# Summing the rows read back behind the last scatter: fp32 products instead of three bf16 parts

## The reference

```python
# layer 2
msg = norm[:, None] * x[col]
agg = jax.ops.segment_sum(msg, row, num_segments=n)
out = relu(agg @ W.T + b)
# layer 3
msg = gate * h[dst] * (cw * mj)[:, None]
agg = jax.ops.segment_sum(msg, src, num_segments=N)
tot = jax.ops.segment_sum(mj, src, num_segments=N)
# after each layer
x = _layernorm(x + layer(x))
```

## Time and profile before

| | |
|---|---|
| median of 3 runs | 16765.21 us (16758.88 to 16766.94) |
| the profiled execution's own time | 16730.78 us |
| its span, first to last instruction | 16728.8 us |
| mean granted TensorE clock | 0.629 |
| PE, DVE, ACT, POOL busy | 71%, 54%, 20%, 74% |

### The profile page before, as it was taken

One profiled execution on the slowest core, in us unless ns is written; L12 is line 12 of the kernel. 1 busy time (PEld: TensorE's weight loads), 2 busy tenths in 40 slices (PEclk: granted clock), 3 DMA queues, 4 the chain that ended last, 5 costly groups with the idle time before them and its releaser, 6 DMA issues. The chain is left out here.

```text
span 16728.8 us, 275034 instructions
## 1 busy us (share of the span) xinstructions
PE 11888.0 (71%) x58162; PEld 10815.9 (65%) x58163; DVE 9022.7 (54%) x22074; ACT 3298.4 (20%) x9767; POOL 12345.1 (74%) x12756
## 2 busy tenths in 40 slices
PE   7777888777666666666533498988853339888884
PEld 6777777777544444444433488888843338888884
DVE  4666667666544444444422266666662226666667
ACT  1111111111211111111111111111123333333332
POOL 4777777777777777777677777777757777777775
PEclk9999999999555555555555555555555555555555
DMA  5444444444333333333211122222221112222222
GB/s 130 101 100 101 101 101 101 100 101 96 87 83 84 86 85 83 86 84 84 66 41 41 48 74 72 75 73 73 74 55 47 47 51 79 78 80 79 78 79 54
DMA packets 1447655, 1320.81 MB, mean 79 GB/s; under 512 B 958662, under 2 KB 1304425, under 8 KB 1443052
## 3 DMA queue, kind: packets, MB, share of 16 engines
q0 software_dynamic: 450320, 493.60, 12.8%
q1 hardware_dynamic: 502094, 520.02, 12.7%
q10 hardware_dynamic: 495148, 306.20, 6.4%
HBM read 903.35 MB, written 415.31 MB: 79 GB/s over the span
## 5 line engine op out<-in xcount | busy, mean ns | idle before, releaser
L1507 POOL DMA_INDIRECT order<-l_msg,l_uring x6250 | 6052.9, 968 | 1918.1 <-issue 1845.9
L1683 PE MATMUL ps<-l_win,l_oht 32*128 x12500 | 2729.9, 413 | 1990.6 <-DMA l_win<-htab 823.3
L1683 PEld LDWEIGHTS ps<-l_win,l_oht 32*128 32x128 f32 x12500 | 2684.1, 327 | 2031.9 <-issue 2031.9
L489 POOL DMA_INDIRECT l_rows<-btab,l_sd x3125 | 3006.0, 962 | 1126.1 <-issue 1084.5
L1027 POOL DMA_INDIRECT l_rows<-y,l_sd x3125 | 2985.7, 955 | 966.5 <-issue 922.3
L1659 PE MATMUL ps<-l_ordb,l_ohs 128*128 128x49 f32 x13600 | 2967.0, 414 | 318.3 <-DVE l_ohs L1552 135.1
L1659 PEld LDWEIGHTS ps<-l_ordb,l_ohs 128*128 128x128 f32 x13600 | 2922.6, 332 | 367.3 <-issue 280.3
L1571 DVE TENSOR_TENSOR acc<-acc,ps 128x49 f32 x7520 | 1525.1, 206 | 1294.5 <-issue 718.6
L630 PE MATMUL ps<-l_rhs,l_lhs 64*128 x6250 | 1422.0, 423 | 676.9 <-DVE l_rows L566 471.8
L630 PEld LDWEIGHTS ps<-l_rhs,l_lhs 64*128 64x128 f32 x6250 | 1350.9, 328 | 738.5 <-issue 738.5
L645 PEld LDWEIGHTS ps<-l_ohe,l_hid 128*128 128x128 f32 x6250 | 1342.9, 332 | 34.9 <-issue 34.1
(11 more groups left out here) (255 smaller groups left out, 11238.0 us busy)
## 6 DMA issues: line engine op xcount, KB each, us to landing
l_ordb<-order SPq DMA_DIRECT2D x752, 250.0 KB
order<-l_msg,l_uring POOLq DMA_INDIRECT x6250
order<-l_zero ACTq DMA_DIRECT2D x125, 775.0 KB, 4.5
l_dstb<-ids SPq DMA_DIRECT2D x376, 200.0 KB
l_eat<-in_ea40P SPq DMA_DIRECT2D x125, 600.0 KB
gates<-l_gate ACTq DMA_DIRECT2D x125, 600.0 KB
l_gin<-gates SPq DMA_DIRECT2D x125, 600.0 KB
l_rows<-btab,l_sd POOLq DMA_INDIRECT x3125
```

Source lines behind the costliest of these rows:

```text
L489: pool.indirect_dma_start(rows[:, t, :], None, d["btab"], bass.IndirectOffsetOnAxis(ap=sd[:, t, 0:1], axis=0)).then_inc(gat[c], 16)
L1507: pool.indirect_dma_start(d["order"], bass.IndirectOffsetOnAxis(ap=uring[:, t:t + 1], axis=0), msg[:, t, :], None).then_inc(sc[c], 16)
L1683: done = t.matmul(look[c][:, j, :], oht[:, c * CE + j * P:c * CE + (j + 1) * P], win[:, ds((w % 2) * SET + c * LW, LW)], start=False, stop ...
```

## The change

The tail uses the functions of the main loop. The split, its four steps on ACT and POOL, their semaphores, the bf16 digits, the bf16 products and SP's separate load are gone. The nine steps run `load_order`, `block_digits`, `block_reduce` and `block_sums`, in the same order on each engine. The main loop isn't touched.

```diff
-        ohsb = [ohs[b][:, 0:RB[b] // 2, :].bitcast(BF16).rearrange("p k (j n) -> p (k j) n", n=P) for b in range(len(RB))]
-        spare = agg[:, 2 * WIDE:pl.NP].bitcast(BF16)
-        parts = [spare[:, 3 * first[b] * MW:3 * (first[b] + RB[b]) * MW].rearrange("p (i k f) -> p i k f", i=3, f=MW) for b in range(len(RB))]
...
@@ sync
-            def load_last(n):
-                ...
-            with sp.Fori(TAIL0, TAIL0 + 1) as n:
+            with sp.Fori(NG - READ0, pl.NS) as n:
                 load_order(n)
-            with sp.Fori(TAIL0 + 1, pl.NS) as n:
-                load_last(n)
@@ gpsimd
-            with pool.Fori(TAIL0, pl.NS) as n:
-                ... less_hi, less_mid
@@ vector
             with dve.Fori(NG - READ0, pl.NS) as n:
-                last_digits(n, 0)
+                block_digits(n, 0)
                 block_sums(n - 1, LAST)
-                last_digits(n, 1)
+                block_digits(n, 1)
                 block_sums(n, 0)
-                last_digits(n, 2)
+                block_digits(n, 2)
                 block_sums(n, 1)
-                last_digits(n, 3)
+                block_digits(n, 3)
                 block_sums(n, 2)
@@ tensor
-            with pe.Fori(TAIL0, pl.NS) as n:
+            with pe.Fori(NG - READ0, pl.NS) as n:
                 for b in range(len(RB)):
-                    last_reduce(n, b)
+                    block_reduce(n, b)
@@ scalar
-            with act.Fori(TAIL0, pl.NS) as n:
-                ... take_hi, take_mid
```

More of the change, by code:

```diff
@@ L1392, in scatter_pass @@
         ohs = [s.sb(f"ohs{b}", [P, RB[b], P]) for b in range(len(RB))]
-        ohsb = [ohs[b][:, 0:RB[b] // 2, :].bitcast(BF16).rearrange("p k (j n) -> p (k j) n", n=P) for b in range(len(RB))]
-        assert all(k % 2 == 0 for k in RB) and 2 * (pl.NP - 2 * WIDE) >= 3 * RT * MW
-        spare = agg[:, 2 * WIDE:pl.NP].bitcast(BF16)
-        parts = [spare[:, 3 * first[b] * MW:3 * (first[b] + RB[b]) * MW].rearrange("p (i k f) -> p i k f", i=3, f=MW) for b in range(len(RB))]
-        hi_made, rest_made, mid_made, lo_made = (s.sem(k) for k in ("hi_made", "rest_made", "mid_made", "lo_made"))
-        TAIL0 = NG - READ0
         ids_in = s.sem("ids_in")
@@ L1552, in block_digits @@
                 v.tensor_tensor(ohs[b][:, :, :], bc(count_row[:, None, :], [P, RB[b], P]), bc(lo, [P, RB[b], P]), ALU.is_equal).then_inc(ohs_ready, 1)
[L1554 to L1559, removed]
             def block_sums(n, b):
@@ L1660, in block_reduce @@
                                     ordb[b][:, k, 0:MW], start=True, stop=True)
[L1661 to L1670, removed]
                 done.then_inc(red_ready, 1)
```

## The result

The changed kernel takes 16723.13 us (median of 14 runs, 16718.25 to 16729.48), against 16758.75 us for the kernel before in 14 runs beside it (16755.34 to 16766.94). The ratio is 0.9978, 95% interval 0.9971 to 0.9985: **36 us faster**. I had forecast 22 us slower, 16787, and a range from 16770 to 16802; the forecast was wrong in sign.

The account below looks back on a forecast made before the run. DVE was taken to bound the tails now, PE after the change. Each tail: 1.73 + 149.45 + 1.6 + 4.63 + 1.77 = 159.2 us against 148.3; twice 10.9 gave 21.8 slower, 16787 us from 16765.21, range 16770 to 16802.

Parts of the forecast that it names:

- PE becomes the tail's bound at 4.27 us a block: Nine steps after the last scatter, layers 2 and 3: fp32 blocks take 4.27 us on PE against DVE's 4.03.
- The clock: TensorE's granted clock in the tails: taken to stay at 0.50, that is 1.2 GHz.
- the rival in which it comes back: Tail at 2.4 GHz: about 2.2 us a block, DVE bounds, time stays 16765; chance 0.06, shared with PE hidden otherwise.
- Four passes of 49 columns, 0.163 us a product: Counter-estimate for tail products: 1.6 us a block, hidden under DVE, time unchanged; the measured block was preferred.
- Closings: PE's pause where the tail's loop closes: 0.2 us a step taken, bounds 0 and 0.68, 8 closings a stage.
- The tail's part: First digits to last adds: 159.2 us a stage against 148.3, 10.9 longer, 21.8 us for both stages.
- Loads of rows, registers: Tail: row reloads hidden by 7 us of slack; address loads need some 1.86 us and have 2.2 at least.
- I cost its removal at nothing, because DVE's adds hide it: Tail: 144 roundings off ACT and 144 subtractions off POOL, some 240 us of work, priced at 0.
- far from the tail: Sign of being wrong: stages far from the tail shift; given no size or chance.
- GpSimd leaves DVE alone: Rival: without POOL's subtractions DVE's tail adds speed up, 29 us, 16736; chance of faster 0.02.

Follow-up runs that it names:

- half of the products: Changed kernel with PE making five of a block's ten products in the nine tail steps: 24334.69 us, ratio 1.0020 to the kernel before.
- the second set: Changed kernel (16701.70 us) and it with unused semaphores (16705.07), memsets (16700.52) or subtractions on POOL (16759.88), beside the kernel before (16733.16).
- the split by additions: Kernel before, its bf16 split kept but ACT negating and POOL adding instead of subtracting: 16678.30 us (ratio 0.9967); at the other pace 24344.22 (1.0020).
- fifth sets: Split by additions (16678.30 us) and changed kernel with eight POOL subtractions in layer 3 alone (16699.69), beside the kernel before (16732.85).

## Why the prediction was wrong

- **PE becomes the tail's bound at 4.27 us a block**: right. Adds that waited for PE in the step above start 4.27 to 4.57 apart, PE is 97% busy, and half of the products free DVE again.
- **The clock**: 0.50 in both tails, with PE 97% busy; the rival in which it comes back is out. The rule that activity releases the halved clock (the Trainium skill, TensorE: Matmul & The Clock Gate, What's actually happening) isn't borne out by these two tails.
- **Four passes of 49 columns, 0.163 us a product** (an estimate from the count of passes in the Trainium skill, FP8 and Floating Point Precision, TensorE Precision Notes): a product took 0.427 us here too (adds at 12289.51 and 12293.78, ten products apart), as the row of before had said.
- **Closings**: 17.43 - 4 x 4.27 = 0.35 a step in layer 2 and 0.45 in layer 3, taken as 0.2. The weight loads pause 0.29 there. With it the tails come to 160.5 and 161.5 for 159.2. They cost 25.4 us for 21.8, and 24 and 27 us where the gathers were slow. The tail's part had the right mechanism and nearly the right size.
- **Loads of rows, registers**: hidden, as forecast; digits behind the first never wait for a load.
- **"I cost its removal at nothing, because DVE's adds hide it"**: this is the step that failed. The 144 subtractions were hidden where they ran. But with them in the program, the gathers of layers 0 and 1 took some 10 ns more each (951 against 941 at least in layer 0), and in those layers POOL is the bound, 6250 times: 51 us in the second set's traces, where I had put nothing. I had looked at what POOL did in the tail and costed nothing outside it; I named a shift "far from the tail" only as what would make me wrong, with no chance and no price. The rival "GpSimd leaves DVE alone" had the right engine and the wrong place and size: DVE's adds still take 2.14 with POOL at rest, and its 29 us aren't the 51 of the gathers. That its 16736 lies near the measured 16723 is luck.
- **Sum**: tails +27, gathers and what follows them -58, together -31 in the second set; -36 in the result.

What isn't settled: how instructions that execute later reach back to the gathers, and how many subtractions it takes, in which of the two stages. Shown is only that the operation counts, and not loop, registers, memsets, semaphores or ACT. Where the instructions' text lies in memory, or what of POOL's own code is made ready for a program, would be guesses. Open too is why the gathers' gain turns into a loss where the index lists arrive late, and what makes the kernel take 24280 us there.

## What to carry to other kernels

Sort an engine's work by where that engine is the bound, not only by where the edit is. If an edit adds or takes away a kind of instruction on POOL, compare the least length of POOL's other instructions in the two traces: nanoseconds on thousands of them outweigh what the edit does in its own place. A pattern that already stands elsewhere in the kernel, as the four fp32 blocks here, prices a stage to a few per cent. And run the pieces apart: a gain of 31 us in the second set was a loss of 27 and a gain of 58 which had nothing to do with the fp32 products, and the split by additions keeps the gain without the loss, at the pace of the second and fifth sets. At the other pace the kernel before was the fastest of the three, so a change of 0.2% is worth having only at the pace at which it was measured.

## What the runs showed of the hardware

- A POOL gather of 128 rows of layer 0 took 940 to 943 ns at least and 946 to 949 in the median in thirteen of the eighteen traces of the experiments, and 951 to 954 and 957 to 960 in the five whose scatter stages of layers 2 and 3 both hold subtractions on POOL. The thirteen include the two with subtractions in layer 3 alone. Scatters took 969 to 972 in the median in both.
- The same kernel took 16733 us in two sets and 24265 to 24294 in three. In the latter POOL waited about 13 us for each group's index list in layer 1, the instructions that open SP's inner loop in layer 0 took 0.70 us instead of 0.04 and 0.05, and the sign of the gathers' effect turned: with the split's work kept, the changed kernel was 60 us faster there (24306.90 against 24366.43), and with subtractions kept 58 us slower in the second set (16759.88 against 16701.70).
- An fp32 product of a 128 x 128 stationary tile and 49 columns took 0.427 us at the 1.2 GHz level, a bf16 one 0.048 (1.43 us for 30 in the tail before). PE was 97% busy with the fp32 ones for 160 us, and the granted clock stayed at 0.50.
